# Second mixture of experts: the eight row scatters of the last batch, one per tile instead of two per tile

## What is computed

```python
x = x + 0.5 * _L0_ffn_ref(_layernorm(x), Wr, br, W1, b1, W2, b2)   # first mixture
x = x + _L0_attn_ref(_layernorm(x), W_Q, W_K, W_V, W_O)            # causal attention
x = x + 0.5 * _L0_ffn_ref(_layernorm(x), Wr, br, W1, b1, W2, b2)   # second mixture
# _L0_ffn_ref: softmax over the two best of 8 router logits; per expert
# y = relu(x @ W1[e] + b1[e]) @ W2[e] + b2[e], weighted and summed
```

## Time and profile before

| | us |
|---|---|
| median of 3 runs | 1075.74 |
| lowest, highest | 1074.48, 1077.14 |
| the profiled execution's own time | 1076.94 |
| its span in the trace | 1075.2 |

### The profile page before, as it was taken

How to read it: one execution, slowest core, us unless ns; L and a number is a source line. 1 busy time by engine, 2 the same in 40 slices (tenths; PEclk the granted TensorE clock), 3 DMA queues, 4 the chain that set the end, 5 groups by cost and what they waited for, 6 DMA issues and landing times.

```text
span 1075.2 us, 24448 instructions
## 1 busy us (share of the span) xinstructions
PE 969.1 (90%) x7675; PEld 817.6 (76%) x7675; DVE 792.5 (74%) x3077; ACT 720.5 (67%) x2044; POOL 282.6 (26%) x326
## 2 busy tenths in 40 slices
PE   7315889987999999999999999999999998988997
PEld 6305889976778778778778778778777776987986
DVE  7513568765877968978978978978978986764657
ACT  2304657654877787787786787787787776766874
POOL 5472320114201101222222222220200202555543
PEclk9957889988999999999999999999999999989999
DMA  9314455632111112211112212211111123444566
GB/s 263 94 58 126 148 160 157 189 101 59 49 31 31 41 31 31 47 42 37 46 42 41 42 42 39 44 42 35 39 36 31 38 67 99 144 124 156 165 208 202
DMA packets 93695, 90.83 MB, mean 84 GB/s; under 512 B 30272, under 2 KB 69344, under 8 KB 93568
## 3 DMA queue, kind: packets, MB, share of 16 engines
q1 hardware_dynamic: 80496, 68.65, 22.6%
q0 software_dynamic: 8512, 18.50, 6.2%
q10 hardware_dynamic: 4560, 2.12, 0.7%
HBM read 64.75 MB, written 24.48 MB: 83 GB/s over the span
## 4 chain that ended last, share of the span: by engine, by line
PE 79%; another core or an unknown queue 6%; DVE 5%; issue 4%; ACT 3%; DMA 1%; SPq 0%; ACTq 0%; DVEq 0%
PE psum L2234 13%; PE psum L2245 13%; PE psum L2191 12%; PE psum L2083 10%; PE psum L2036 7%; PE psum L2034 7%; PE psum L2035 6%; PE psum L2253 6%; PE psum L2046 2%; PE psum L1947 1%; PE psum L2056 1%; ACT arena L879 1%; ACT arena L815 1%; DVE y_sb L1580 1%
## 5 line engine op out<-in xcount | busy, mean ns | idle before, releaser
L936 ACT ACTIVATE arena<-arena,neg_max 128x512 f32<-128x512 f32 (+3 forms) x512 | 281.8, 559 | 1.6 <-issue 1.6
L1699 DVE CUSTOM_DVE_ANT_0 arena<-psum,causal 128x512 f32<-128x512 f32 (+3 forms) x512 | 217.1, 482 | 3.7 <-PE psum L2191 3.7
L944 ACT ACTIVATE arena<-psum 128x512 f32<-128x512 f32 x192 | 103.9, 597 | 154.9 <-PE psum L2234 154.6
L2083 PE MATMUL psum<-w_sb,arena 128*128 x1192 | 155.1, 281 | 14.1 <-issue 9.1
L879 ACT ACTIVATE arena<-psum,b_t 128x256 f32<-128x256 f32 (+1 forms) x332 | 125.3, 455 | 52.3 <-PE psum L2036 29.0
L2083 PEld LDWEIGHTS psum<-w_sb,arena 128*128 128x128 f32 x1192 | 146.4, 198 | 16.7 <-issue 16.5
L2234 PE MATMUL psum<-ident,arena 128*128 128x128 f32 x1280 | 155.5, 275 | 3.7 <-ACT arena L944 1.8
L2245 PE MATMUL psum<-arena 128*64 128x512 f32 (+3 forms) x1024 | 152.0, 439 | 0.7 <-DVE arena L1712 0.7
L2234 PEld LDWEIGHTS psum<-ident,arena 128*128 128x128 f32 x1280 | 141.8, 142 | 9.3 <-ACT arena L944 3.5
L739 POOL DMA_INDIRECT arena<-y_tiles,y_at x64 | 60.8, 950 | 316.5 <-PE psum L2191 204.0
L2245 PEld LDWEIGHTS psum<-arena 128*64 128x64 f32 x1024 | 68.0, 136 | 83.9 <-issue 74.1
(11 more groups left out here) (311 smaller groups left out, 1950.7 us busy)
## 6 DMA issues: line engine op xcount, KB each, us to landing
w_raw<-in_L_ffn_W_dram SPq DMA_DIRECT2D x66, 256.0 KB
arena<-inv_dram SPq DMA_DIRECT2D x128, 128.0 KB
xg<-x_slots SPq DMA_DIRECT2D x55, 144.0 KB
arena<-in_L_ffn_W_dram SPq DMA_DIRECT2D x17, 256.0 KB
arena<-y_rows SPq DMA_DIRECT2D x16, 256.0 KB, 3.4
y_tiles<-y_sb SPq DMA_DIRECT2D x27, 128.0 KB, 1.7
x_slots<-blank SPq DMA_DIRECT2D x18, 144.0 KB
out_dram<-xs ACTq DMA_DIRECT2D x8, 256.0 KB
```

Source lines behind the costliest of these rows:

```text
L936: ins = act.activation(prob_tile(i, h, t), prob_tile(i, h, t), ACT.Exp, scale=-1.0, bias=neg_max[i % 2][:, h, t:t + 1], accum_out=row_sum[ ...
L944: act.activation(four_turned(g), turned_bank(i, g), ACT.Copy).then_inc(pt_act, 1)
L1699: ins = dve.tensor_tensor_reduce(out=prob_tile(i, h, t), in0=score_tile(t, h), in1=causal[:, SEQ - (t + 1) * P:SEQ], scale=-1.0, scalar=-2 ...
L2083: ins = pe.matmul(Y_BANKS[side(f, n)][:, r * D:(r + 1) * D], h_t[side(f, n)][:, k, r * P:(r + 1) * P], w2_sb[:, bass.ds(e * (CHUNKS * D) + ...
```

## The change

The condition that picks the tile for scatter j changes. Before, scatters 0 to 7 go behind the results of tiles 9, 9, 10, 10, 11, 11, 12, 13. Now they go behind tiles 9, 10, 11, 12, 13, 14, 15, 16. Their number, sizes and order among themselves stay, and no wait is added or removed.

```diff
                 for j in range(TOP * QT):
-                    if n == LAST_PUT_AT + max(j // 2, j - 3):
+                    if n == LAST_PUT_AT + j:
                         put(U1 + 7, j % TOP, j // TOP, x_put[7])
```

## The result

The change makes the kernel slower by about a third of a percent. Over 17 runs each the median is 1077.79 us against 1074.48 us before; the ratio is 1.0032, with a 95% interval from 1.0016 to 1.0048, that is +1.7 to +5.2 us. The prediction said 1077.2 us, range 1073.0 to 1081.0, slower. It reckoned +1.5 us from a median of 1075.74 over 3 runs; over 17 runs the kernel before has a median 1.3 us lower, and the change adds 3.3 us by the medians.

A forecast was written before the change was run, and what follows sets the result against it. PE was taken as the bound, busy 969.1 of 1075.2 us, losing time only where it stands still. Tile 21's later load (+1.5 us) and neutral runs (0), on a median of 1075.74, gave 1077.2 us, range 1073.0 to 1081.0.

The forecast's parts named there:

- What bounds tile 21: Before the change, PE idles 3.25 us ahead of tile 21 because its row load waits for the blank writes, not the scatters.
- The last scatter becomes what ends last: On SP's wait ahead of tile 21's rows, the eighth scatter ends last, issuing the load 1.39 to 1.66 us later.
- PE's gap of 4.75 us: PE's idle time ahead of tile 21's transposes was to grow from 3.25 us to 4.75 us.
- The sum of +1.5 us: Whole forecast loss: the later load of tile 21 adds 1.5 us on PE's path, POOL's runs add 0.
- the fall of the clock behind the gap: Rival: PE's clock falls at the longer gap ahead of tile 21, costing up to 3.4 us, giving 1080.6 us; chance 0.22.
- The late load: Tile 21's row load, held by the last scatter, is issued about 1.5 us later, wholly on PE's path.
- The most likely case: The forecast itself: +1.5 us from tile 21's load, POOL's runs neutral, no clock fall; 1077.2 us, chance 0.40.
- no change: Whole-kernel outcome within 0.3%, 3.2 us, of the time before; chance 0.52.
- slower: Whole-kernel outcome slower by over 0.3%; chance 0.34.
- The runs are neutral: Recutting POOL's strings of indirect DMAs moves PE's gaps to tiles 14 to 17 at 0 us, ends -7.8 and about +3.4.
- the rival of the shorter runs: Shorter strings of POOL's DMAs cut PE's first idle stretch, saving 1.8 us plus 3.4 of clock: 1072.0 us; chance 0.16.
- The rival in which POOL never pauses: 24 indirect DMAs follow each other over eight tiles, adding a 3.4 us stretch at tiles 14 to 17: 1080.6 us; chance 0.12.

The follow-up runs named there:

- late15: The kernel before with only the last scatter moved, from behind tile 13 to behind tile 15; 1072.93 us against 1073.63, ratio 0.9991.
- before_again: The kernel before, unchanged, traced once more on the chip where its median is 977.89 us; 977.68 us.
- all9: The kernel before with all eight scatters behind tile 9; 978.25 us against 977.89, ratio 1.0002.
- blanks_before: The kernel before, scatters unmoved, with SP sending the blank writes in pairs behind the row loads of tiles 17 to 20; 1065.16 us against 1064.86, ratio 0.9999.
- blanks_again: A repeat of blanks_before (early blank writes, old scatters) against the kernel before; 1064.64 us against 1066.28, ratio 0.9990.
- late16: The kernel before with only the last scatter moved, from behind tile 13 to behind tile 16; 1068.95 us against 1064.86, ratio 1.0039.
- after: The changed kernel in its first trace, scatters behind tiles 9 to 16, against the kernel before; median 1077.79 us against 1074.48, ratio 1.0032.
- after_again: The changed kernel, unchanged, run once more against the kernel before; 1068.41 us against 1066.28, ratio 1.0029.
- blanks_after: The changed kernel with the blank writes sent early, in pairs behind the row loads of tiles 17 to 20; 1068.61 us against 1064.86 before, ratio 1.0024.
- late17: The kernel before with only the last scatter moved, from behind tile 13 to behind tile 17; 986.29 us against 977.89, ratio 1.0088.
- paused: The kernel before with each scatter followed on POOL by two writes that nobody reads; 983.78 us against 977.89, ratio 1.0060.
- paused1: The kernel before with each scatter followed on POOL by one write that nobody reads; 1066.23 us against 1066.28, ratio 0.9997.

## Why the prediction was right, and where its sizes were off

- **What bounds tile 21** before: right as to what ends last. The load waits for the blank writes; late15, before_again and all9 show the same kind of gap with the last scatter as early as tile 9 and as late as tile 15. But it is 1.52 to 1.68 us long there, not 3.25, and taking it away (blanks_before, blanks_again) brought no time clear of the spread.
- **The last scatter becomes what ends last:** right, and shown by single edits (late16 alone gives the loss, late15 gives none). From its start to the load I took 2.92 to 3.19 us from the earlier trace rows; six traces have 2.47, 2.48, 2.48, 2.87, 2.97 and 3.41. The rows held within 0.5 us. The Trainium skill (DMA: Bandwidth & Descriptors, "Anatomy of one DMA — SWDGE (gpsimd) path") gives 2.0 us plus the bytes; an estimate by it is 2.2 us for these 128 rows of 576 bytes, which these traces do not confirm as the time up to the load: all six are longer. (My rows are 0.7 to 1.0 us above that estimate; the 0.9 to 1.2 in the prediction are against its fixed part alone.)
- **PE's gap of 4.75 us:** too long as a single number. It was 2.42 us in the first trace of the change and 3.98 in the second, since PE itself came later to tile 21. The load shifts with POOL's queue, which shifts with the results of tiles 15 and 16, so the scatter's lateness is not simply added. The distance from tile 20 to 21 tells it better: 7.1 to 7.6 us in the four traces with the last scatter behind tile 16, against 6.9 in the first trace of before, from which the 1.5 us were reckoned, and 5.1 to 5.3 in the three others that wait for the blanks with PE standing still.
- **The sum of +1.5 us was the mis-sized term.** It was 3.4 us in the result (by the ratio; 3.3 by the medians), 3.1 in the repetition and 4.2 in late16. What I had set apart as a rival with a chance of 0.22, the fall of the clock behind the gap, was there behind tile 21's gap in each of the six traces in which the eighth scatter held the load (after, late16, after_again, blanks_after, late17, paused: granted clock 0.54 to 0.67), and behind it in none of the others; the 4.4 us of blanks_again and paused1 is a short wait on DVE in each. It costs 1.5 to 2.5 us there (21 to 22 in 5.0 to 6.0 us, not 3.5), less than the 3.4 us that I gave it. The late load and the fall are one mechanism, not two cases: the predicted 1.5 and the measured 1.5 to 2.5 of the fall give 3.0 to 4.0, and the three runs measure 3.1 to 4.2. That this fits so well is not a test of the 1.5: reckoned from the short gaps of late15, before_again and all9, the late load alone is 1.8 to 2.5 us. Both pieces stood in the working; the step that failed was to take the likeliest case as the one without the fall although the trace already had a fall at a gap of 3.84 us.
- **The forecast of 1077.2 us came within 0.6 us of the measured 1077.79 partly by luck.** The change cost 3.3 us by the medians where 1.5 were forecast, and the longer series put the kernel before 1.3 us lower. The most likely case held the clock up, and it fell; the rival with the fall, at 1080.6, had the mechanism but too high a price. By the prediction's own measure the outcome, +0.32%, lies on its border of 0.3% between "no change" (0.52) and "slower" (0.34).
- **The runs are neutral:** no loss or gain from them is shown, and neither is the reason given for it. The first stretch does get shorter with one scatter a tile (7.5 to 8.9 us in four traces against 10.1 to 10.7 in five), as the rival of the shorter runs had it, but on the average the tiles behind give it back: from 14 to 20 the four take 35.2, 34.0, 29.3 and 29.0 us, the five 32.2, 30.5, 32.2, 32.2 and 31.8. With one trace of each, differences of 3 us either way can be chance. The rival in which POOL never pauses did not come about: it paused for 4.95 and 2.45 us, and the run of eight or more that the prediction saw from 982 to 990 was one of six. That the runs cause the gaps was my reading of a coincidence, and all9 speaks against it in that form. What causes them stays open; they were there in every group of runs but that of the chip with 977.89 us, and of the experiments none removes them.

## What to carry to other kernels

Before a transfer is moved later, look up who waits for its completion and what ends last there now: here the last scatter lay hidden behind another wait; two tiles later was free within the spread, the third cost 4 us. Where a wait on the path grows past the gaps that the trace shows at full clock, count the work behind it at half clock as part of the same case. And a stretch of idle time that no row explains is not to be put on the price list of an edit until another chip has shown it too.

## What was not expected of the hardware

- The same kernel runs at a median of 977.89 us on one chip and at 1064.86 to 1074.48 us on others. Between the two traces of it the spans differ by 99 us. Some 73 us of these are idle time of PE (33 us against 106), much of which the profile gives no reason for (PE waits for ACT or DVE, and these wait for a releaser that the profile does not know); the other 26 are a longer busy time (942.9 against 969.1 us) at a mean granted clock of 0.964 instead of 0.999. One mark tells the traces apart: in the ten with such gaps ACT and DVE together sit idle for 121 to 151 us, in 27 to 36 waits put down to `remote`; in the four of the chip with 977.89 us no wait is. The longest two of the first trace of before (engine, tile, line, what it waited for: us in total, times, longest):

```profile
ACT wo_t L839 <- remote: 28.8, 1, 28.8
...
DVE place L1179 <- remote: 23.3, 1, 23.3
```

  Who releases them is not shown; it would be the next thing to look for.
- The clock held at gaps of PE of 1.52, 1.67, 1.68 and 3.25 us ahead of tile 21 and fell at 2.42, 3.73, 3.92, 3.98, 5.61 and 8.38 us; the 2.42 us gap was preceded by further stops of PE, so the length of one gap alone does not decide. Behind it one tile took 5.0 to 6.0 us where 3.5 is usual.
